# The twelve half-row products of an attention step in another order

## What is computed

```python
q = _rope(split_heads(x @ Wq + bq))
k = _rope(split_heads(x @ Wk + bk))
v = split_heads(x @ Wv + bv)
scores = einsum('bhqd,bhkd->bhqk', q, k) / sqrt(16)
probs = softmax(scores, axis=-1)
out = einsum('bhqk,bhkd->bhqd', probs, v)
return out @ Wo + bo
```

## Time and profile before

| | |
|---|---|
| median of 3 runs | 3463.47 us (3461.51 to 3465.16) |
| the profiled execution's own time | 3460.53 us |
| its span | 3458.8 us |
| PE busy | 3288.3 us, 95% |
| DVE busy | 3242.6 us, 94% |
| ACT busy | 2701.5 us, 78% |
| POOL busy | 810.4 us, 23% |
| mean granted TensorE clock | 0.989 |

### The profile page before, as it was taken

The page is one execution under the profiler, slowest core; times in us unless marked ns, Lnnn a source line. Parts: engine busy times, 40 slices in busy tenths (PEclk is TensorE's granted clock), DMA queues, the critical chain, the costliest instruction groups (busy, mean ns, idle before and its releaser), DMA issues.

```text
span 3458.8 us, 59198 instructions
## 1 busy us (share of the span) xinstructions
PE 3288.3 (95%) x22596; PEld 1189.6 (34%) x22596; DVE 3242.6 (94%) x4953; ACT 2701.5 (78%) x4973; POOL 810.4 (23%) x698
## 2 busy tenths in 40 slices
PE   7777778979999999999999999999999999999999
PEld 3222222533333333333333333333333333333334
DVE  7999998589999999999999999999999999999943
ACT  5766666747888888888888888888888888888865
POOL 2899997752000000000000000000000000000004
PEclk9999999979999999999999999999999999999999
DMA  2000001142012020202020211202020202020011
GB/s 66 1 10 1 0 1 55 49 125 31 14 27 31 10 33 6 33 8 34 6 33 6 33 18 24 32 7 33 6 33 8 34 6 33 6 34 8 7 55 49
DMA packets 53677, 87.09 MB, mean 25 GB/s; under 512 B 13200, under 2 KB 40464, under 8 KB 49232
## 3 DMA queue, kind: packets, MB, share of 16 engines
q1 hardware_dynamic: 53200, 82.77, 12.6%
q10 hardware_dynamic: 192, 0.52, 0.1%
HBM read 53.37 MB, written 21.23 MB: 22 GB/s over the span
## 4 chain that ended last, share of the span: by engine, by line
PE 82%; DVE 11%; issue 4%; ACT 1%; POOL 0%; DMA 0%; SPq 0%; DVEq 0%; POOLq 0%; ACTq 0%
PE banks L1487 29%; PE banks L1444 16%; PE banks L1439 15%; PE banks L1402 11%; DVE arena L989 5%; PE banks L522 3%; DVE arena L958 3%; PE banks L1400 2%; PE banks L785 1%; DVE arena L969 1%; DVE arena L1660 1%; PE banks L187 1%; PE banks L777 1%; PE banks L1509 1%; PE banks L1498 0%
## 5 line engine op out<-in xcount | busy, mean ns | idle before, releaser
L1643 DVE TENSOR_REDUCE arena<-banks 128x1 f32<-128x512 f32 x4032 | 2504.2, 684 | 19.0 <-PE banks L1402 15.6
L1617 ACT ACTIVATE arena<-banks 128x512 f32<-128x512 f32 x4096 | 2114.9, 603 | 417.6 <-PE banks L1439 409.7
L1439 PE MATMUL banks<-arena 64*128 64x512 bf16 x4032 | 1246.6, 380 | 0.0
L1444 PE MATMUL banks<-arena 35*128 35x512 bf16 x4032 | 1207.9, 378 | 0.9 <-DMA arena<-max_rows 0.5
L1487 PE MATMUL banks<-arena 128*32 128x512 f32 x8192 | 1090.8, 605 | 0.0
L1400 PE MATMUL banks<-arena 64*128 64x512 bf16 x2048 | 789.4, 387 | 22.9 <-DVE arena L1660 20.2
L1402 PE MATMUL banks<-arena 64*128 64x512 bf16 x2048 | 787.4, 386 | 0.6 <-DVE arena L1643 0.6
L1439 PEld LDWEIGHTS banks<-arena 64*128 64x128 bf16 x4032 | 375.9, 93 | 392.0 <-PE banks L1444 7.9
L1402 PEld LDWEIGHTS banks<-arena 64*128 64x128 bf16 x2048 | 188.0, 92 | 796.6 <-DVE arena L1643 792.3
L1444 PEld LDWEIGHTS banks<-arena 35*128 35x128 bf16 x4032 | 357.6, 93 | 158.7 <-ACT arena L1617 9.5
L685 PE MATMUL banks<-arena 128*128 128x512 f32 x512 | 258.1, 628 | 107.4 <-DVE arena L958 107.2
(11 more groups left out here) (133 smaller groups left out, 1653.8 us busy)
## 6 DMA issues: line engine op xcount, KB each, us to landing
arena<-qk_parts SPq DMA_DIRECT2D x242, 128.0 KB, 7.1
qk_parts<-arena SPq DMA_DIRECT2D x32, 384.0 KB, 2.6
arena<-arena SPq DMA_DIRECT2D x63, 128.0 KB, 2.3
x_res<-in_x SPq DMA_DIRECT2D x8, 512.0 KB, 7.4
arena<-in_trig SPq DMA_DIRECT2D x2, 2048.0 KB, 8.1
arena<-qk_parts SPq DMA_DIRECT2D x64, 64.0 KB, 10.1
att_t<-arena SPq DMA_DIRECT2D x128, 32.0 KB
arena<-att_t SPq DMA_DIRECT2D x8, 512.0 KB, 5.3
```

Of the source, the lines that this page charges most:

```text
L1439: return nc.tensor.matmul(sc[:, (4 * t + j) % SB, :], k, q, start=(j == 1), stop=(j != 1))
L1444: return nc.tensor.matmul(sc[:, (4 * t + j) % SB, :], k, q, start=(j != 1), stop=(j == 1))
L1617: nc.scalar.activation(prob[:, t % PBUF, j * CH:(j + 1) * CH], sc[:, n % SB, :], ACT.Exp, scale=SCALE).then_inc(exp_done, 1)
L1643: nc.vector.tensor_reduce(part_max[:, b % 2, u // NC, u % NC:u % NC + 1], mx[:, unit_bank(b, u), :], AXX, ALU.max).then_inc(dve_read, 1)
```

## The change

In `step`, the calls stand in another order. Nothing else is touched; the products, their waits, their banks and their semaphores are the same.

```diff
@@ -1532,12 +1532,12 @@
             first_half(nh, nt, 0)
             first_half(nh, nt, 1)
             max_stream(b, u + 1)
+            second_half(nh, nt, 0)
             first_half(nh, nt, 2)
-            second_half(nh, nt, 0)
+            max_stream(b, u + 2)
             first_half(nh, nt, 3)
-            max_stream(b, u + 2)
+            second_half(nh, nt, 2)
             second_half(nh, nt, 1)
-            second_half(nh, nt, 2)
             second_half(nh, nt, 3)
             max_stream(b, u + 3)
             if t > 0:
```

## The result

The changed kernel takes 3470.43 us in the median of 17 runs (3466.74 to 3474.80), the one before 3463.08 us in 17 runs beside them (3458.57 to 3466.24). The ratio is 1.0025, with a 95% interval of 1.0018 to 1.0031. That is 8.7 us slower (0.0025 x 3463; the interval is 6.2 to 10.7 us, and the two medians lie 7.4 us apart), where 17.6 us was forecast.

What follows compares the result with a forecast made beforehand. The prediction took a loop through TensorE and VectorE, 1.17 + 0.31 + 1.00 = 2.48 us a step, as the bound. With 0.02 us more in 881 steps, 3463.5 + 17.6 = 3481 us, range 3460 to 3492 us.

Steps and rivals of the forecast that it cites:

- What bounds the kernel before: A 2.48 us loop through TensorE and VectorE: m3 waits for m0's reduction, with TensorE ready 0.03 to 0.07 us earlier.
- f2 behind s0, the second of a pair, 0.47 to its release: f2 queued behind s0 starts at +0.48 and releases s2 0.47 later, so s2's load comes at +0.95.
- two sizes: Waits from a first half's start to its second half's load: 0.47 as second of a starting pair, otherwise 0.43 to 0.44.
- m3 at +1.19 instead of +1.17: s1 at +0.96 frees the high rows 0.23 later, so m3 starts 0.02 us later than VectorE allows.
- The end of the loop (0.31 + 1.00) follows it unchanged: From m3 to `weigh` 0.31 us and on to the next m0 1.00, so the step grows by m3's full 0.02.
- 881 steps of 0.02 are 17.6 us: Total loss over ordinary steps, those without row maximum or transposition; effects in those other steps, 0.6 us each way, cancel.
- This is the costly move: s1, on m3's half of the rows, queued behind waiting s2, starts at +0.96 instead of +0.88.
- the third rival: Waits add up: late releases delay both s3 and m3, m3 at +1.22, 44 us slower, 3508 us; chance 0.08.
- The first rival: f2 releases s2 after 0.44, s2's load at +0.92, m3 stays at VectorE's +1.17: 3463.5 us; chance 0.26.

Runs made afterwards that it cites:

- the halved maxima: VectorE reduces only 256 of the 512 keys of each maximum: ratio 0.9861 in the order before, 1.0015 in the changed order.
- changed with s1 back: The changed order with only s1 put back ahead of s2: ratio 1.0034, from 5 runs.
- both kernels without the increment: s0's semaphore increment left out, first exponential waiting on f2's: ratio 1.0014 in the changed order, 1.0000 with s0 before f2 as only reorder.

## Why the prediction was off

- *What bounds the kernel before*: right, and shown by the halved maxima. TensorE was ready for m3 at +1.105, 0.067 ahead of VectorE, and the step could end 0.044 sooner, since s3 is then the last; 0.03 to 0.07 of slack was given.
- *f2 behind s0, the second of a pair, 0.47 to its release*: right within a hundredth (+0.48 for f2; the load of s2 at +0.957, 0.95 forecast). That the extra time goes with the place in the pair was a choice between two sizes, which the rows didn't prove; moving f0 ahead of m0, and leaving out an increment, show it.
- *m3 at +1.19 instead of +1.17*: right in the changed kernel (1.191 against 1.172).
- *"The end of the loop (0.31 + 1.00) follows it unchanged"*: this step failed, and it is the term that was mis-sized. From m3 to `weigh` it was 0.317 before and is 0.308 after. The table shows on what this depends: where m3's weights are loaded right ahead of it (load and product 0.004 apart), `weigh` comes 0.316 or 0.317 behind m3 whenever m3 sets it (before, changed with s1 back, both kernels without the increment, f0 ahead of m0). Where the load was 0.014 or 0.015 ahead (changed, and changed with half maxima), it is 0.308. And s3, loaded early, sets `weigh` after 0.306 where it is last (half maxima in the order before; s0 ahead of f2). Before, m3 was loaded late because its bank was. In the changed kernel its load doesn't wait for a bank but its product waits for the rows, so the weights are in. Half of the 0.019 by which m3 is late is given back there: the step grows by 0.010, not 0.02.

  The changed kernel's own trace shows both cases side by side. In its steps with a row maximum m3's bank comes free later, and m3's load comes 0.004 ahead of its product. Here is one, with m0 at 2028.82, PEld first and then PE:

```profile
2030.01 0.09 PEld L1400 LDWEIGHTS banks<-arena 64*128 64x128 bf16 x1
```

```profile
2030.01 0.39 PE L1400 MATMUL banks<-arena 64*128 64x512 bf16 x1
2030.33 1.06 PE L1487 MATMUL banks<-arena 128*32 128x512 f32 x8
```

  In 18 of these steps m3 starts at +1.191 or before, no later than in the ordinary ones, and `weigh` comes at +1.506 in the median, not at +1.499. So it is the load's lead and not the start of m3 that makes the difference. Why the lead counts isn't shown.

  The rows had this in them: a product without an early load is recorded with 0.39 and followed after 0.22 to 0.23, one with an early load with 0.37 to 0.38 and followed 0.01 sooner. I used it for f2 and not for m3.
- *881 steps of 0.02 are 17.6 us*: 877 x 0.010 = 8.8 us. (The steps with whole products at the end are 17, not 16; the count of 1007 has this right.) The steps with a row maximum give back 0.008 each (2.517 to 2.509), where 0.01 was said, and those with a transposition cost 0.006 (2.677 to 2.683), where up to 0.01 was. The trace has 7.3 us in all. Some of what is left is that two late transfers cost the execution before 1.2 us (steps of 3.27 and 2.86 us), while the changed one met one, in a step of 2.82.
- *"This is the costly move"*, of s1 behind s2: wrong as well. Undone in the changed order, and done alone in the one before, it moves nothing. m3 was late by two paths of almost the same length: behind s1 on its rows, and behind s3's load in the queue. I had worked out the one and left the other to the third rival. The costs are those of s0 ahead of f2 (0.006 a step) and m2 ahead of f3 (0.004).
- The first rival (no change) asked for the 0.03 not to come with f2; it did. The third needed both delays on one path; they lie on two.

## What to carry to other kernels

When two engines are both full, look for the loop that passes through both, and time it from start to start; a change of order within one engine shows only once it exceeds what the other's wait hides, here 0.044 us of a step. Don't let two products that both raise a semaphore end at the same moment if the later one in program order is waited for; a queue with nothing between a product and the one that it releases cost nothing here once that was avoided. And when a delay is carried along a chain, carry with it whether each link's weights are loaded early: here that was half of the answer.

## What was not expected of the hardware

- Two products on the two halves of the rows that end together raise their semaphores one after the other. The one later in program order is late by 0.024 us (the load of s2 at 0.957 with s0's increment, 0.933 without), and the shift is 0.030 for m0's reduction when m0 is the later one (0.454 against 0.424 after its start). Program order decides, not the order of starts: f3, ahead of m2 in the queue but started 0.004 behind it, releases s3 in 0.432; behind it in the queue, in 0.463. The 26.3 ns an increment in the Trainium skill ("TensorE: Matmul & The Clock Gate", "The cost: per-tile semaphore tail") fits within 0.01.
- Whether the weights of the last product are loaded right ahead of it or earlier moves what follows on all rows by 0.008 to 0.009 us (`weigh` 0.316 to 0.317 behind m3 against 0.308), within one trace too. A late start is so partly paid by an early load.
- A transposition over all rows behind a half-row product started 0.32 us after it, in f0 ahead of m0.
